# Film feed-forward in halves of tokens with its biases added on DVE, and a grouped-attention projection rotated in halves with copies spread over three engines

## The reference

```python
scale_out, shift_out = jnp.split(c_t @ W_film_out + b_film_out, 2, axis=-1)
y = y * (1.0 + mod_gate * scale_out) + mod_gate * shift_out
xt = x_text + y
h = layernorm(xt, g_ffn, b_ffn)
h = jax.nn.gelu(h @ W1 + b1, approximate=False) @ W2 + b2
xt = xt + h
return layernorm(xt, g_norm_out, b_norm_out)
...
h = rmsnorm(x, ln1_w)
q = (h @ Wq + bq).reshape(batch, seq, NQ, HD)
k = (h @ Wk + bk).reshape(batch, seq, NKV, HD)
v = (h @ Wv + bv).reshape(batch, seq, NKV, HD)
q = rmsnorm(apply_rope(q, cos, sin), qn_w)
k = rmsnorm(apply_rope(k, cos, sin), kn_w)
```

## Time and profile before

| | |
|---|---|
| median of 3 runs | 1891.41 us (1890.3 to 1895.34) |
| profiled execution, its own time | 1896.19 us |
| its span, first to last instruction | 1894.4 us |
| mean granted PE clock | 0.874 |
| PE busy | 81% of the span |
| DVE busy | 70% |
| ACT busy | 49% |
| POOL busy | 37% |
| feed-forward of the film block | 1419.36 to 1463.28 us |
| grouped projection | 1464.42 to 1514.54 us |

### The profile page before, as it was taken

The page is one execution under the profiler, slowest core; times in us unless marked ns, Lnnn a source line. Parts: engine busy times, 40 slices in busy tenths (PEclk is TensorE's granted clock), DMA queues, the critical chain, the costliest instruction groups (busy, mean ns, idle before and its releaser), DMA issues. The chain is left out here.

```text
span 1894.4 us, 20029 instructions
## 1 busy us (share of the span) xinstructions
PE 1526.4 (81%) x6681; PEld 814.2 (43%) x6737; DVE 1318.5 (70%) x3033; ACT 926.9 (49%) x1448; POOL 697.9 (37%) x526
## 2 busy tenths in 40 slices
PE   5776998999867468788878878887574399999798
PEld 2223443455435124455445545555453233333555
DVE  5997677565274599989999899898474646664233
ACT  5664114656213117777777777788211045554121
POOL 1765111121000008887888888788200200000012
PEclk8898999999878678998989898898777579999599
DMA  5000110000092200000000000000200200000000
GB/s 134 1 1 13 51 51 3 1 1 0 17 199 45 58 0 1 1 1 1 1 1 1 1 1 1 1 1 1 84 8 16 72 1 1 1 1 1 0 1 11
DMA packets 30244, 37.14 MB, mean 20 GB/s; under 512 B 13543, under 2 KB 23371, under 8 KB 29007
## 3 DMA queue, kind: packets, MB, share of 16 engines
q1 hardware_dynamic: 28586, 23.96, 4.6%
q10 hardware_dynamic: 1544, 11.79, 3.1%
HBM read 29.50 MB, written 6.24 MB: 19 GB/s over the span
## 5 line engine op out<-in xcount | busy, mean ns | idle before, releaser
L1472 PE MATMUL psum<-film_ka,film_context_qa 97*128 97x512 bf16 (+1 forms) x832 | 342.7, 413 | 145.7 <-DVE search_and_weigh_kept L1667 64.0
L1844 ACT ACTIVATE search_and_weigh_e<-psum,search_and_weigh_bias 128x512 f32<-128x512 f32 (+1 forms) x416 | 268.0, 666 | 111.2 <-PE psum L1474 107.3
L1667 DVE MAX8 search_and_weigh_kept<-psum 128x8 f32<-128x171 f32 (+2 forms) x1216 | 317.7, 324 | 5.0 <-PE psum L1474 3.8
L1474 PE MATMUL psum<-film_kb,film_context_qb 128*128 128x512 bf16 (+1 forms) x777 | 318.2, 410 | 0.0
L1693 DVE SCALAR_TENSOR_TENSOR search_and_weigh_e<-psum,film_context_top,search_and_weigh_e 128x512 f32<-128x512 f32 (+1 forms) x283 | 201.0, 717 | 37.5 <-ACT search_and_weigh_e L1844 35.1
L1715 POOL TENSOR_TENSOR search_and_weigh_e<-search_and_weigh_e,search_and_weigh_keep 128x512 f32<-128x512 f32 (+1 forms) x133 | 150.7, 1133 | 167.9 <-ACT search_and_weigh_keep L1823 165.0
L1472 PEld LDWEIGHTS psum<-film_ka,film_context_qa 97*128 97x128 bf16 x832 | 92.2, 111 | 253.4 <-DVE search_and_weigh_e L1693 99.2
L2678 DVE TENSOR_REDUCE gqa_attend_low<-psum 128x1 f32<-128x128 f32 (+7 forms) x128 | 96.6, 757 | 84.2 <-PE psum L2602 83.8
L2889 POOL TENSOR_TENSOR residual<-residual,top_expert_kept 128x1024 f32<-128x1024 f32 x8 | 18.7, 2344 | 357.1 <-DVE top_expert_kept L2862 357.1
L1749 PEld LDWEIGHTS psum<-ctx_rows,search_and_weigh_mean_T 128*128 128x128 f32 (+1 forms) x816 | 131.8, 207 | 32.8 <-issue 6.0
L1719 POOL TENSOR_TENSOR search_and_weigh_mean<-search_and_weigh_e 128x512 f32<-128x512 f32 (+1 forms) x104 | 134.1, 1290 | 12.3 <-DVE search_and_weigh_e L1693 5.1
(11 more groups left out here) (551 smaller groups left out, 2767.2 us busy)
## 6 DMA issues: line engine op xcount, KB each, us to landing
film_kb<-film_k_rows ACTq DMA_DIRECT2D x4, 1601.0 KB
film_ka<-film_k_rows ACTq DMA_DIRECT2D x3, 1601.0 KB
ctx_T<-in_ctx_T SPq DMA_DIRECT2D x1, 2401.5 KB
gqa_experts_w<-in_L_ffn_W SPq DMA_DIRECT2D x1, 2048.0 KB
film_convolve_back<-in_dft_back SPq DMA_DIRECT2D x1, 1728.0 KB, 13.1
film_k_rows<-cross_attention_film_hi SPq DMA_DIRECT2D x6, 256.0 KB, 2.0
film_k_rows<-cross_attention_film_mid SPq DMA_DIRECT2D x6, 256.0 KB, 2.0
film_k_rows<-cross_attention_film_low SPq DMA_DIRECT2D x6, 256.0 KB, 2.0
```

Source lines behind the costliest of these rows:

```text
L1472: pe.matmul(out, a["qa"][0:ROWS, h, rows], a["ka"][0:ROWS, h, c + b:c + b + cols], start=True, stop=False)
L1474: last = pe.matmul(out, a["qb"][:, h, rows], a["kb"][:, h, c + b:c + b + cols], start=False, stop=True)
L1667: last = dve.max(kept[:, h % 2, first + s, :], bank[:, lo:hi])
L1844: act.activation(e[:, n % RING, sub, 0:PIECES[u][1]], ps[:, SEARCH_BANKS + q % WEIGH_BANKS, 0:PIECES[u][1]], ACT.Exp, bias=bias[:, i % 2, ...
```

## The change

In `film_convolve` ACT multiplies by the gate while it copies film_out, and POOL, in a program of its own, adds the shift half of it to xn (`moved`).

In `film_out_ffn` DVE forms (film_out+1)*y in one instruction and adds `moved`. The hidden layer is made in eight units, four feature chunks for the first half of the tokens and then four for the second, each of 512 columns and in one of four banks that are used in turn; a unit that uses a bank again waits for its gelu. ACT's gelu works unit by unit. The output of a half is begun when its four units are there, without a matmul for the bias. b2 is loaded to all partitions, and DVE adds it to xt, and the shift of the last norm to x, before it waits for PE; it adds the two halves of the output separately.

In `gqa_project` the bias matmuls are left out; DVE adds the bias, loaded to all partitions, while it takes two tiles at a time out of PSUM, and ACT's copies go away. Rotation and squares are made for tiles 0 to 3 and then for tiles 4 to 7. The weights of queries and keys are multiplied in by POOL, after the squares. POOL begins its nine copies when the first of the three parts is there, in the order of the parts; ACT makes five of the nine copies of the query heads and DVE four.

```diff
...
+            act.wait_ge(rows_loaded, 16 * 4)
             for n in range(2):
                 act.activation(a["film_out"][:, 4 * n:4 * n + 4], ps[:, 4 + 2 * n:6 + 2 * n, :].rearrange(
-                    "p b (i s d) -> p (b i) s d", s=2, d=D), ACT.Copy).then_inc(out_copied, 1)
+                    "p b (i s d) -> p (b i) s d", s=2, d=D), ACT.Copy, scale=a["gate"][:, 0:1]).then_inc(out_copied, 1)
...
+        @block.gpsimd
+        def _(pool):
+            pool.wait_ge(out_copied, 2)
+            pool.tensor_tensor(a["moved"][:], a["film_out"][:, :, 1, :], g["xn"][:], ALU.add)
...
+    def u_bank(unit):
+        return ps[:, U_FIRST + unit % U_BANKS, :]
...
+                             (w2[:], t["L1_xattn_W2"].rearrange("(q p) d -> p q d", p=P)),
+                             (b2[:], broadcast_row("L1_xattn_b2", t)),
...
             link = chained(dve, chain_dve)
-            link(film_apply(dve, link, a["film_out"][:], a["gate"], a["y"][:], scale, xt[:]))
-            link(dve.tensor_tensor(xt[:], xt[:], g["xn"][:], ALU.add))
+            link(dve.scalar_tensor_tensor(out=xt[:], in0=a["film_out"][:, :, 0, :], scalar=1.0, in1=a["y"][:],
+                                          op0=ALU.add, op1=ALU.mult))
+            link(dve.tensor_tensor(xt[:], xt[:], a["moved"][:], ALU.add))
             normalise(dve, link, xt, norm[0]["stats"], norm[0]["mv"], norm[0]["rstd"], var_ready[0],
                       root_ready[0], h, h_ready)
-            dve.wait_ge(out_done, 1)
-            link(dve.tensor_tensor(xt[:], xt[:], ps[:, 4:6, :].rearrange("p b (i d) -> p (b i) d", d=D),
-                                   ALU.add))
+            dve.wait_ge(loaded, 16 * N_LOADS)
+            link(dve.tensor_tensor(g["x"][:], g["x"][:], tiles(shift[:]), ALU.add))
+            link(dve.tensor_tensor(xt[:], xt[:], tiles(b2[:]), ALU.add))
+            for n in range(2):
+                rows = slice(4 * n, 4 * n + 4)
+                dve.wait_ge(out_done, n + 1)
+                link(dve.tensor_tensor(xt[:, rows], xt[:, rows], ps[:, 6 + n, :].rearrange("p (i d) -> p i d", d=D),
+                                       ALU.add))
             normalise(dve, link, xt, norm[1]["stats"], norm[1]["mv"], norm[1]["rstd"], var_ready[1],
                       root_ready[1], h, normed)
             dve.wait_ge(normed, NT)
-            dve.wait_ge(loaded, 16 * N_LOADS)
             link(dve.tensor_tensor(h[:], h[:], tiles(gain[:]), ALU.mult))
-            link(dve.tensor_tensor(h[:], h[:], tiles(shift[:]), ALU.add))
             link(dve.tensor_tensor(g["x"][:], g["x"][:], h[:], ALU.add))
...
-            for q in range(NH_):
-                act.wait_ge(u_done, q + 1)
-                b = 2 * ((q + 1) % 4)
-                act.activation(act_T[:, q, :], ps[:, b:b + 2, :].rearrange("p b n -> p (b n)"),
-                               ACT.Gelu, bias=b1[:, q:q + 1]).then_inc(act_ready, 1)
+            for unit in range(2 * NH_):
+                n, q = divmod(unit, NH_)
+                act.wait_ge(u_done, unit + 1)
+                act.activation(act_T[:, q, n * HALF:(n + 1) * HALF], u_bank(unit), ACT.Gelu,
+                               bias=b1[:, q:q + 1]).then_inc(act_ready, 1)
...
             transpose_tiles(pe, h, g["ident"][:], ps, h_ready, hT_psum)
             pe.wait_ge(loaded, 16 * N_LOADS)
-            pe.wait_ge(hT_ready, 2)
-            for q in range(NH_):
-                for n in range(2):
-                    last = pe.matmul(ps[:, 2 * ((q + 1) % 4) + n, :], w1[:, q * P:(q + 1) * P],
-                                     hT[:, n * HALF:(n + 1) * HALF], start=True, stop=True)
-                last.then_inc(u_done, 1)
-            pe.wait_ge(act_ready, NH_)
-            for i in range(NT):
-                out = ps[:, 4 + i // 4, (i % 4) * D:(i % 4 + 1) * D]
-                for q in range(NH_):
-                    pe.matmul(out, act_T[:, q, i * P:(i + 1) * P], w2[:, q, :], start=q == 0, stop=False)
-                last = pe.matmul(out, g["ones"][:, 0:P], b2[:], start=False, stop=True)
-            last.then_inc(out_done, 1)
+            for unit in range(2 * NH_):
+                n, q = divmod(unit, NH_)
+                if q == 0:
+                    pe.wait_ge(hT_ready, n + 1)
+                if unit >= U_BANKS:
+                    pe.wait_ge(act_ready, unit - U_BANKS + 1)
+                pe.matmul(u_bank(unit), w1[:, q * P:(q + 1) * P], hT[:, n * HALF:(n + 1) * HALF], start=True,
+                          stop=True).then_inc(u_done, 1)
+            for n in range(2):
+                pe.wait_ge(act_ready, NH_ * (n + 1))
+                for i in range(4 * n, 4 * n + 4):
+                    for q in range(NH_):
+                        last = pe.matmul(ps[:, 6 + n, (i % 4) * D:(i % 4 + 1) * D], act_T[:, q, i * P:(i + 1) * P],
+                                         w2[:, q, :], start=q == 0, stop=q == NH_ - 1)
+                last.then_inc(out_done, 1)
...
+    ACT_COPIES = (0, 1, 2, 3, 4)
...
+            for dst, src in ((w[:], t["L1_Wqkv"]), (bias[:], t["L1_bqkv"].to_broadcast([P, WQKV])),
...
-            dve.wait_ge(qkv_ready, 4)
...
-            link(dve.tensor_tensor(low, x1, c, ALU.mult))
-            link(dve.tensor_tensor(high, x1, s, ALU.mult))
-            for n, (out, op) in enumerate(((low, ALU.subtract), (high, ALU.add))):
-                dve.wait_ge(half_ready, n + 1)
-                link(dve.tensor_tensor(out, out, half[:, n], op))
+            dve.wait_ge(loaded, 16 * N_LOADS)
+            for n in range(2):
+                half_rows = slice(4 * n, 4 * n + 4)
+                for b in range(2 * n, 2 * n + 2):
+                    dve.wait_ge(qkv_done, 2 * (b + 1))
+                    dve.tensor_tensor(qkv[:, 2 * b:2 * b + 2].rearrange("p i h c -> p i (h c)"),
+                                      ps[:, 4 + b, 0:2 * WQKV].rearrange("p (i n) -> p i n", i=2),
+                                      bias[:].unsqueeze(1).to_broadcast([P, 2, WQKV]), ALU.add).then_inc(qkv_ready, 1)
+                dve.wait_ge(qkv_ready, 2 * (n + 1))
+                x1 = qkv[:, half_rows, 0:HQK, 0:HH]
+                c = cos[:, half_rows].unsqueeze(2).to_broadcast([P, 4, HQK, HH])
+                s = sin[:, half_rows].unsqueeze(2).to_broadcast([P, 4, HQK, HH])
+                low, high = turned[:, half_rows, :, 0:HH], turned[:, half_rows, :, HH:HD]
+                dve.tensor_tensor(low, x1, c, ALU.mult)
+                link(dve.tensor_tensor(high, x1, s, ALU.mult))
+                for k, (out, op) in enumerate(((low, ALU.subtract), (high, ALU.add))):
+                    dve.wait_ge(half_ready, 2 * n + k + 1)
+                    dve.tensor_tensor(out, out, half[:, k, half_rows], op).then_inc(turned_ready, 1)
+                dve.wait_ge(turned_ready, 2 * (n + 1))
+                rows = turned[:, half_rows]
+                link(dve.tensor_tensor(square[:, 4 * n * HQK:4 * (n + 1) * HQK].rearrange("p (i h) c -> p i h c", h=HQK),
+                                       rows, rows, ALU.mult))
             flat = turned[:].rearrange("p i h c -> p (i h) c")
-            link(dve.tensor_tensor(square[:], flat, flat, ALU.mult))
             dve.reduce_sum(scale[:], square[:], AX).then_inc(square_ready, 1)
             dve.wait_ge(scale_ready, 1)
             link(dve.reciprocal(scale[:], scale[:]))
+            dve.wait_ge(weighted, 2)
             link(dve.tensor_tensor(flat, flat, scale[:].unsqueeze(2).to_broadcast([P, NT * HQK, HD]), ALU.mult))
-            for w_n, lo, hi in ((qn_w, 0, HQ), (kn_w, HQ, HQK)):
-                v = turned[:, :, lo:hi, :]
-                link(dve.tensor_tensor(v, v, w_n[:].unsqueeze(1).unsqueeze(1).to_broadcast(
-                    [P, NT, hi - lo, HD]), ALU.mult))
-            link(dve.tensor_copy(part[:, 0], turned[:]))
+            dve.tensor_copy(part[:, 0], turned[:]).then_inc(part_ready, 1)
+            dve.wait_ge(part_ready, 1)
             link(dve.tensor_tensor(rest[:], turned[:], part[:, 0], ALU.subtract))
-            link(dve.tensor_copy(part[:, 1], rest[:]))
-            dve.tensor_tensor(part[:, 2], rest[:], part[:, 1], ALU.subtract).then_inc(parts_ready, 1)
-            dve.wait_ge(parts_ready, 1)
-
+            dve.tensor_copy(part[:, 1], rest[:]).then_inc(part_ready, 1)
+            dve.wait_ge(part_ready, 2)
+            dve.tensor_tensor(part[:, 2], rest[:], part[:, 1], ALU.subtract).then_inc(part_ready, 1)
+            dve.wait_ge(part_ready, 3)
             for n in range(9):
-                cols = slice(n * HD, (n + 1) * HD)
-                last = dve.tensor_copy(a["split"][:, :, 0:HQ, cols], part[:, n // 3, :, 0:HQ, :])
-            last.then_inc(stacked, 1)
-            dve.wait_ge(stacked, 10)
+                if n not in ACT_COPIES:
+                    cols = slice(n * HD, (n + 1) * HD)
+                    dve.tensor_copy(a["split"][:, :, 0:HQ, cols], part[:, n // 3, :, 0:HQ, :])
...
-            pool.wait_ge(qkv_ready, 4)
```

(40 more changed lines are left out.)

20 lines of the change are left out of this document (7 added, 13 removed).

## The result

| | before | after |
|---|---|---|
| median | 1891.81 us (4 runs, 1890.3 to 1895.34) | 1868.78 us (4 runs, 1860.97 to 1871.93) |
| ratio, with its 95% interval | | 0.9869 (0.9835 to 0.9903) |
| profiled execution, its own time | 1896.19 us | 1871.93 us |
| its span | 1894.4 us | 1870.1 us |

The changed kernel is 23.0 us faster by the medians and 24.3 us by the profiled executions. The forecast was 1868.0, from a sum of 23.5 us. First the page of after, which answers to the earlier trace rows: engines' busy time, and the granted clock in 40 slices.

A forecast was written before the change was run, and what follows sets the result against it. A nearly serial chain of about 96 us, feed-forward and projection, was taken to bound the kernel. 11.0+10.2+0.2+2.1=23.5 us off the 1894.4 us span gave 1870.9, or 1868 for the median; range 1861 to 1876.

The forecast's parts named there:

- Feed-forward: FiLM block's feed-forward: earlier head, hidden units by halves, output without bias matmuls and a shorter tail save 11.0 us.
- Projection up to the sum of squares: Grouped attention's projection, first matmul to end of reduction: 13.7 us instead of 23.94, 10.2 us saved.
- (c): Rival: clock rises early in feed-forward and even projection, copies do not meet; 4 to 5 us more, 1863.5; chance 0.12.
- Weights: Projection, reduction's end to first subtraction: POOL's weight products beside root and reciprocal make 5.78 us 5.6, 0.2 saved.
- Copies: Projection, first subtraction to PE's first head: 9.1 us instead of 11.18, 2.1 saved; 4.6 or 0 as bounds.
- (d): Attention behind the projection warms up later, costing some 2.5 us: 1865 to 1872; counted within the forecast's chance of 0.70.
- (e): Rival: attention's clock stays at half for long; past 59 us the kernel is slower, 1897 or more; chance 0.02.
- (b): Rival: feed-forward stays at half clock as smaller units stop for gelu; its gain -0.8, not 11.0: 1880; chance 0.04.
- (a): Rival: DVE and POOL meet worse in projection, half rotations 4 to 5 us, copies bring nothing; 7 us less, 1875; chance 0.10.

The follow-up runs named there:

- feed-forward alone: Changed kernel with the old `gqa_project`, so only the feed-forward's part of the change (with the gate in the copy and POOL's add); 1885.76 us, 0.9941 of before.
- copies on DVE: Changed kernel with all nine query copies on DVE and none on ACT, POOL still starting with the first part; 1869.83 us.
- all grouped: Changed kernel with one-row bias matmuls issued ahead of the products in `film`, attention gate and output, and the experts' router; 1845.58 us, 0.9746 of before.

## Why the prediction held, point by point

- **Feed-forward, 11.0 us predicted, 11.1 measured** (the stage lasted 45.06 us and now 33.92, and began 0.07 later). xt was ready at 1421.91, where 1421.90 was forecast; POOL's addition ran from 1396.51 to 1398.86, before DVE's work at 1399.47, and was hidden; ACT's scaled copies took 2.12 instead of 1.94, hidden too. First hidden matmul 1427.66 (1427.65); second product 1436.39, 7.31 us long (1436.5, 7.1); last addition done at 1444.50 (1444.55). Gelu took the 0.69 us that was guessed, and the clock rose 3.6 us after the first matmul where 4.0 was assumed. How close the sum came is partly luck: from the first hidden matmul to the end of the second addition after needs 16.84 us, and the same code needs 15.75 (feed-forward alone) to 17.13 (copies on DVE) in other kernels, where the clock rose at another moment. The loads were called free, and were in after, but with little to spare: in the experiment with b2 on PE again DVE waited 0.18 us for the last of them, and ACT's first copy of hT began 1.93 us after the transposes instead of 1.35, so PE lost 0.6.
- **Projection up to the sum of squares, 10.2 predicted, 10.9 measured.** The term that was furthest off is PE's: 5.25 us at half speed were put for 16 records and they took 3.88, since the clock rose within them. Little of it reached the path, as half 0 was ready after 3.18 us instead of 3.4. With the one-row matmuls back the clock stays at half for all 15 us, so taking them off gave the clock as well; the main sum has no such term, and only (c) names it. A half rotation took 2.76 us where 3.0 was put, twice 0.24. With 0.2 from the one and 0.5 from the other, 13.7 became 13.07. What the forecast missed is a question of credit: it counted the early start of half 0 as part of the gain, and the whole rotation does as well.
- **Before the first matmul of the projection** 0.18 us were lost (9.92 from the block's start instead of 9.74), where the forecast had nothing. Most of it lies in DVE's second step of the norms (2.00 and 1.93 instead of 1.89 and 1.82, beside POOL's memset). Why is open, but the edits of `gqa_project` don't make it: the kernel with the old projection has 2.00 and 1.93 too, and the one with the new projection alone 1.88 and 1.82.
- **Weights, 0.2 predicted, 0.20 measured.** The reciprocal stayed at 1.15 us beside POOL, so the other outcome (a loss of 0.3, if POOL held it up) did not come. The prediction drew it from the Trainium skill, but the section that it cites, "Who interferes with whom" of SBUF — State Buffer, names DVE operations with two SBUF inputs, and the reciprocal has one; the trace agrees with the page.
- **Copies, 2.1 predicted, 2.8 measured.** 0.29 us of hold behind each of DVE's three operations was put in; DVE's cast took 0.95 instead of 0.83, its subtractions 1.49 and 1.58 instead of 1.49 twice. That is 0.2 us in place of 0.9, and nearly all of the difference.
- **Sum.** 11.07-0.18+10.87+0.20+2.78=24.74 us up to PE's first turn; forecast 23.5. The span gave 24.3, so 0.4 went lost behind. The attention's clock rose 0.9 us later after the first turn than before, which at half speed is 0.4 us and would be all of it: that is (d), a sixth of the size that it was given. (e) and (b) did not come. (a) fell with the 2.76 and the 0.95, and its sum was off as well: half rotations of 4 to 5 us rather than 3 cost 1 to 2 each, not the 2.3 that was put in; (c) came in part: the early clock in the projection and cheaper copies are in it, worth 0.2 and 0.7 on the path, not 4 to 5.

The medians differ by 23.0 and not 24.3 us. That is within the spread of after's own runs, 1860.97 to 1871.93. Where this spread comes from is open: stages that no edit touched differ by several microseconds between executions. The phase of the clock in them could do it, but no run here isolates it.

## What to carry to other kernels

Don't add a bias with a one-row matmul behind each tile. Put it into an addition that DVE has time for, or group it into full banks while PE is idle, or give it 128 rows. Ask then what the stage waits for next: in `film` that was soon DVE. Working in halves pays where an engine stands still for the other half (3.3 us in the feed-forward), and pays nothing where the first engine is done in 4 us and the second has over 8 us of work behind it (the projection). When unaltered stages move by up to 8 us between executions, judge an edit by the interval between two events of its own stage.

## What was not expected of the hardware

The granted clock fell to half while PE showed no gap at all, when records of one row alternated with full ones, or stood in a row of eight: in after at 1380 in `film`, and at 1728 in the gate product (0.56 over 1728 to 1730, 0.50 up to 1734). It stayed at 1.00 with 128 rows in their place. Fewer one-row records did not lower it at once: in the kernel with all grouped it was 1.00 behind four of them (1712.51 to 1714.42) and fell at about 1719.7, after four more from 1716.40; and with two beside eight full ones, in the feed-forward with b2 on PE, it was 1.00 from 1438 to 1450. Where the border lies, no run here shows. The Trainium skill, TensorE: Matmul & The Clock Gate (section "Part 1: The HAM clock gate"), says that the gate goes by how busy PE has been recently. The trace does not agree, if busy is taken as the profile's busy time: with PE busy for 2.00 of 2.00 us the clock fell.

DVE and POOL shared their ports better than feared. The Trainium skill, SBUF — State Buffer (section "Who interferes with whom"), says that DVE operations with two SBUF inputs and POOL operations that read SBUF contend. The trace agrees for long operations (a product of 640 elements 1.89 us beside POOL, 0.82 alone), but beside POOL's copies of 256 elements DVE's subtraction of 1280 took 1.49 to 1.58 us, against 1.49 alone.
